# A quantiser's scale search beside a GRU recurrence: four groups of four scales, one for each step, without GpSimd

## The reference

```python
# layer 0: h from a GRU over the 32 steps, then attention on h, then a ternary-weight FFN
def cell(h, x):
    gi = x @ W_ih + b_ih
    gh = h @ W_hh + b_hh
    r = sigmoid(i_r + h_r); z = sigmoid(i_z + h_z)
    n = tanh(i_n + r * h_n)
    return (1.0 - z) * n + z * h

# layer 1, last part: both weights quantised to 5 bits, in blocks of 64 along the input
SHRINKS = np.linspace(0.4, 1.0, 16)
def mse_quant_dequant(w):
    amax = max(|wb|) per block;  base = max(amax, 1e-8) / 15
    for s in SHRINKS:
        scale = base * s
        deq = clip(round(wb / scale), -15, 15) * scale
        err = sum((deq - wb) ** 2)          # per block; the scale with the least error is kept
    return clip(round(wb / best_scale), -15, 15) * best_scale
```

## Time and profile before

| | us |
|---|---|
| median of 3 runs | 1633.81 (1633.55 to 1635.8) |
| the profiled execution | 1636.86 |
| its span | 1634.7 |

### The profile page before, as it was taken

The page is one execution under the profiler, slowest core; times in us unless marked ns, Lnnn a source line. Parts: engine busy times, 40 slices in busy tenths (PEclk is TensorE's granted clock), DMA queues, the critical chain, the costliest instruction groups (busy, mean ns, idle before and its releaser), DMA issues.

```text
span 1634.7 us, 24270 instructions
## 1 busy us (share of the span) xinstructions
PE 1419.8 (87%) x7971; PEld 1003.5 (61%) x7986; DVE 1108.2 (68%) x2613; ACT 867.6 (53%) x1772; POOL 367.8 (22%) x287
## 2 busy tenths in 40 slices
PE   5888888877998989899999886878889898989897
PEld 2333333345786877777777674555667585766766
DVE  3788888861455656564646668848686867678685
ACT  3877776756657565656666555443443424343311
POOL 2655554521211212121212100000102020110102
PEclk9999998888999999999999997979899999999999
DMA  9222222214110101010111131000000000000000
GB/s 368 53 52 52 52 77 52 52 53 147 52 33 26 40 26 39 26 38 26 38 38 61 40 136 65 1 26 7 13 8 13 6 13 6 13 7 7 14 7 13
DMA packets 26019, 73.45 MB, mean 45 GB/s; under 512 B 3928, under 2 KB 4700, under 8 KB 24544
## 3 DMA queue, kind: packets, MB, share of 16 engines
q1 hardware_dynamic: 25520, 71.67, 13.8%
q10 hardware_dynamic: 432, 0.92, 0.2%
HBM read 49.50 MB, written 23.07 MB: 44 GB/s over the span
## 4 chain that ended last, share of the span: by engine, by line
PE 37%; issue 20%; DVE 13%; ACT 5%; POOL 5%; POOLq 0%; DVEq 0%; ACTq 0%
PE psum L924 8%; PE psum L895 6%; POOL stats L1710 4%; PE psum L573 4%; PE psum L934 3%; DVE work L1809 2%; PE psum L680 2%; PE psum L619 2%; ACT probs_t L1507 2%; PE psum L841 2%; PE psum L606 1%; PE psum L875 1%; PE psum L987 1%; PE psum L907 1%; PE psum L848 1%
## 5 line engine op out<-in xcount | busy, mean ns | idle before, releaser
L573 PE MATMUL psum<-h_all,w_big 128*128 (+1 forms) x1024 | 246.2, 387 | 6.6 <-ACT ident_bf L1218 4.9
L573 PEld LDWEIGHTS psum<-h_all,w_big 128*128 128x128 f32 x1024 | 190.4, 193 | 43.1 <-issue 14.0
L1710 POOL TENSOR_TENSOR stats<-stats,minus_half 128x32 f32<-128x32 f32 x15 | 103.5, 6902 | 369.3 <-ACT stats L1251 369.3
L1809 DVE SCALAR_TENSOR_TENSOR work<-work,taps 128x248 f32<-128x248 f32 (+30 forms) x558 | 151.1, 349 | 0.0
L531 PE MATMUL psum<-w_big,h_all 128*64 128x512 f32 x512 | 133.0, 643 | 0.0
L924 PE MATMUL psum<-w_big 128*128 128x256 f32 x448 | 114.8, 416 | 20.1 <-ACT w_big L1536 20.1
L924 PEld LDWEIGHTS psum<-w_big 128*128 128x128 f32 x448 | 92.6, 210 | 42.2 <-ACT w_big L1536 26.6
L1809 DVE SCALAR_TENSOR_TENSOR h_all<-h_all,taps 128x248 f32<-128x248 f32 (+30 forms) x434 | 116.0, 344 | 0.0
L895 PE MATMUL psum<-work,w_big 128*128 128x256 f32 x512 | 115.8, 379 | 0.0
L680 PE MATMUL psum<-w_big,gru_mem 128*128 128x256 f32 x512 | 113.6, 379 | 0.0
L1679 POOL TENSOR_TENSOR work<-work,ffn_mem 128x512 f32<-128x512 f32 x60 | 85.6, 1458 | 95.2 <-DVE work L1876 90.1
(11 more groups left out here) (283 smaller groups left out, 2830.2 us busy)
## 6 DMA issues: line engine op xcount, KB each, us to landing
value_rows<-w_emb SPq DMA_DIRECT2D x128, 128.0 KB, 2.3
work<-value_rows SPq DMA_DIRECT2D x16, 1024.0 KB, 5.6
w_big<-in_Wq SPq DMA_DIRECT2D x2, 2048.0 KB, 16.7
w_big<-in_Wo SPq DMA_DIRECT2D x2, 2048.0 KB, 21.0
out<-w_big SPq DMA_DIRECT2D x16, 256.0 KB, 2.0
x_res<-out SPq DMA_DIRECT2D x15, 256.0 KB, 2.7
work<-in_w SPq DMA_DIRECT2D x1, 2048.0 KB, 11.7
w_big<-in_Wv SPq DMA_DIRECT2D x1, 2048.0 KB, 18.8
```

Source lines behind the costliest of these rows:

```text
L573: mm = pe.matmul(bank(n % 2)[:, o * TA:(o + 1) * TA], w_big[:, s, k * H * HD + at:k * H * HD + at + HD], h_all[:, k, bass.ds(i * BA, BA), ...
L1710: pool.tensor_tensor(qk_r, qk_ms, minus_half[:, 0:2 * GA * HU], ALU.pow).then_inc(r_on.sem, 1)
L1809: ins = dve.scalar_tensor_tensor(dst[:, :, lag:], src[:, :, :T - lag], tap, dst[:, :, lag:], ALU.mult, ALU.add)
```

## The change

The 16 scales are tried in four groups of four, so that each GRU step begins a group; group n (of 32) is raised in step n, rounded and subtracted in step n+1, squared in step n+2 and summed in step n+3. All 16 subtractions are VectorE's one-operation kind, all squares are ScalarE's; `scaled` and `squared` are gone, and GpSimd keeps `times_base` and `times_scale`. `w5_abs` has two buffers, `w5_tmp` four. `piece_out` is cut into five parts that are spread over steps 2, 3 and 0; parts 1 and 3 stand between the candidate's argument and the wait for its tanh. `piece_in(0)` comes before the first step's update, with a DMA of its own for the first eighth of w5, and a wait for the rest and for the constants (const_in) follows the first step. The hardware loops of three engines become straight code. The last two pieces of w5, not the last alone, are worked in gru_mem. The two bf16 constants are made in step 4. After the recurrence the last squares stand between the copies of projections, the raw weights are loaded earlier (the third when all errors are summed), and the three sums of absolute values come before `chunk(0)`, into scratch.

```diff
-GROUPS = (range(0, 6), range(6, 11), range(11, 16))
-BY_DVE = (2, 1, 1)
+GROUP = 4
+NG = NS // GROUP
+GROUPS = PIECES * NG
-W5_PARTS = (0, 4), (4, 7), (7, 8)
+W5_PARTS = (0, 4), (4, 6), (6, 8)
...
@@ SyncE
-            sp.dma_start(w5, io["w5"]).then_inc(w5_in, 16)
+            sp.dma_start(w5[:, 0:PC], io["w5"][:, 0:PC]).then_inc(w5_first_in, 16)
+            sp.dma_start(w5[:, PC:], io["w5"][:, PC:]).then_inc(w5_in, 16)
...
-            for pair in (T // 2 - 2, T // 2 - 1):
-                store_values(pair)
+            store_values(T // 2 - 2)
+            sp.wait_ge(h_on.sem, T)
+            sp.wait_ge(h_kept.sem, T)
+            for j, src in enumerate(("w_gate", "w_up", "w_down")):
+                if j == 2:
+                    sp.wait_ge(shr_err.sem, GROUPS)
+                sp.dma_start(raw[j], io[src]).then_inc(raw_in, 16)
+            store_values(T // 2 - 1)
             for j in range(2):
                 sp.wait_ge(v_out[j], 16 * T * V_TILES // 2)
+            load_values(0, 0, 0)
             sp.dma_start(w_emb[:], io["W_emb"]).then_inc(emb_in, 16)
-            sp.wait_ge(shr_err.sem, 3 * PIECES - 2)
-            load_values(0, 0, 0)
+            sp.dma_start(x_in_buf, io["x_tok"][:, 0:GA, :]).then_inc(x_in, 16)
             store_w5(2)
-            sp.wait_ge(h_on.sem, T)
-            sp.wait_ge(h_kept.sem, T)
-            for dst, src in zip(raw, ("w_gate", "w_up", "w_down")):
-                sp.dma_start(dst, io[src]).then_inc(raw_in, 16)
-            sp.dma_start(x_in_buf, io["x_tok"][:, 0:GA, :]).then_inc(x_in, 16)
@@ ScalarE
+            def raised(n, parts):
+                q, g = n // NG, n % NG
+                if 0 in parts:
+                    act.wait_ge(shr_pre.sem, q + 1)
+                    if q:
+                        act.wait_ge(shr_err.sem, n - NG + 1)
+                for j in parts:
+                    ins = act.activation(w5_tmp[g][:, j, :], w5_abs[q % 2], ACT.Identity, bias=magic_col[:],
+                                         scale=float(1.0 / SHRINKS[g * GROUP + j]))
+                if GROUP - 1 in parts:
+                    ins.then_inc(shr_raised.sem, 1)
+
+            def squares(n):
+                act.wait_ge(rest_on.sem, n + 1)
+                act.activation(w5_tmp[n % NG], w5_tmp[n % NG], ACT.Square).then_inc(sq_on.sem, 1)
+
+            for t in range(T):
+                u = t - 1
+                act.wait_ge(hid_sum.sem, t + 1)
+                act.activation(gates, bank(t % 2)[:, RZ], ACT.Tanh, scale=0.5).then_inc(rz_on.sem, 1)
+                if t:
+                    raised(t, range(0, 1))
+                act.wait_ge(cand_in.sem, 2 * t + 2)
+                act.activation(cand, cand, ACT.Tanh).then_inc(cand_on.sem, 1)
+                if u >= 2:
+                    keep_values(u // 2 - 1, u % 2)
+                if t:
+                    raised(t, range(1, 2))
...
+                if t == 0:
+                    absolute(0)
+                    raised(0, range(0, 2))
+                raised(t, range(2, GROUP))
+                if t >= 2:
+                    squares(t - 2)
+                if t % NG == NG - 1 and t < T - 1:
+                    absolute(t // NG + 1)
+                if t == NG:
+                    act.wait_ge(const_in, 16 * 5)
+                    act.activation(mask_bf[:], mask, ACT.Copy)
+                    const_on.raised_by(act.activation(ident_bf[:], ident[:], ACT.Copy))
...
-            act.wait_ge(shr_err.sem, 3 * PIECES - 1)
-            keep_qk(0, range(QK_TILES))
+            keep_qk(0, range(0, 2))
+            squares(GROUPS - 2)
+            keep_qk(0, range(2, 4))
+            squares(GROUPS - 1)
+            keep_qk(0, range(4, QK_TILES))
+            act.wait_ge(raw_in, 16 * 3)
+            sum_raw(0)
             keep_values(T // 2 - 1, 0)
+            act.wait_ge(shr_err.sem, GROUPS)
             keep_sums(0)
+            sum_raw(1)
             keep_values(T // 2 - 1, 1)
-            act.wait_ge(shr_err.sem, 3 * PIECES)
+            sum_raw(2)
             chunk(0, False, False)
@@ GpSimd
+            for q in range(3):
+                times_base(q)
+            for q in range(3, PIECES):
+                times_scale(q - 3)
+                if q >= late:
+                    pool.wait_ge(hid_sum.sem, (q - late + 1) * PC // B + 1)
+                times_base(q)
+            for q in range(PIECES - 3, PIECES - 1):
+                times_scale(q)
@@ VectorE
+            def errors(n):
+                g = n % NG
+                dve.wait_ge(sq_on.sem, n + 1)
+                dve.tensor_reduce(err[:, g * GROUP:(g + 1) * GROUP, :].rearrange("p s b -> p (s b)"),
+                                  blocks(w5_tmp[g].rearrange("p j n -> p (j n)")), AX.X, ALU.add).then_inc(shr_err.sem, 1)
+
+            def round_off(n):
+                q, g = n // NG, n % NG
+                dve.wait_ge(shr_raised.sem, n + 1)
+                dve.tensor_scalar(w5_tmp[g], w5_tmp[g], MAGIC + QMAX, MAGIC, ALU.min, ALU.subtract).then_inc(shr_cut.sem, 1)
+                dve.wait_ge(shr_cut.sem, n + 1)
+                for j in range(GROUP):
+                    tmp = w5_tmp[g][:, j, :]
+                    ins = dve.scalar_tensor_tensor(tmp, w5_abs[q % 2], -float(1.0 / SHRINKS[g * GROUP + j]), tmp,
+                                                   ALU.mult, ALU.add)
+                ins.then_inc(rest_on.sem, 1)
+
+            for t in range(T):
+                u = t % 2
+                q = t // NG
+                if t == 0:
+                    dve.wait_ge(w5_first_in, 16)
+                    piece_in(0)
+                dve.wait_ge(rz_on.sem, t + 1)
...
+                if t % NG == 3 and q >= 1:
+                    piece_out(q - 1, 1)
+                elif t % NG == 0 and q >= 2:
+                    piece_out(q - 2, 3)
...
+                if 3 <= t < T - 1:
+                    errors(t - 3)
+                if t:
+                    round_off(t - 1)
+                if t == 0:
+                    dve.wait_ge(w5_in, 16)
+                    dve.wait_ge(const_in, 16 * 5)
...
+                if t % NG == 0 and q >= 2:
+                    piece_out(q - 2, 4)
+                if t % NG == 1 and q < PIECES - 1:
+                    piece_in(q + 1)
+                if t % NG == 2 and q >= 1:
+                    piece_out(q - 1, 0)
+                if t % NG == 3 and 1 <= q < PIECES - 1:
+                    piece_out(q - 1, 2)
+            round_off(GROUPS - 1)
+            errors(GROUPS - 4)
+            errors(GROUPS - 3)
...
-            errors(PIECES - 1, 2)
-            dve.wait_ge(w5_on.sem, PIECES - 1)
-            piece_out(PIECES - 1)
+            for part in range(2, 5):
+                piece_out(PIECES - 2, part)
+            errors(GROUPS - 2)
+            errors(GROUPS - 1)
+            for part in range(5):
+                piece_out(PIECES - 1, part)
             chunk(0, False, False)
```

296 lines of the change are left out of this document (76 added, 220 removed).

## The result

| | before | after |
|---|---|---|
| median of 4 runs each, us | 1634.8 (1633.55 to 1640.75) | 1564.43 (1561.26 to 1571.89) |
| the profiled execution, us | 1636.86 | 1571.89 |
| its span, us | 1634.7 | 1570.1 |
| first operation of step 4 | 54.15 | 46.91 |
| a piece, (step 28 less step 8) / 5 | 41.3 | 35.02 |

The ratio is 0.9569 with a 95% interval of 0.9526 to 0.9612.

The account below looks back on a forecast made before the run. VectorE's queue was taken to bound the GRU stage, much of its busy time being stretching beside GpSimd. Gains of 46.1 us (stage) and 8.1 (hand-over), together 54.2, gave a median of 1579.6 us, range 1570 to 1598.

Parts of the forecast that it names:

- VectorE's own work: GRU stage: VectorE's undisturbed queue takes 7.71 us a step plus 4.4 a piece, 35.2 us a piece.
- the price of GpSimd's remaining work: GRU stage: each of GpSimd's two remaining products a piece delays VectorE 0.4 us, making 36.0 us a piece.
- my low end: Whole kernel: 1570 us, with remaining GpSimd work free (5.6 less) and no wait for the weights (3.7 less).
- The start: First GRU steps: base and GpSimd's product precede step 0; step 1 at 25.4 us, step 4 at 48.0.
- TensorE's pace: Rival, GRU stage: TensorE's clock falls in each step, making it 9.4 us; 11 us more, 1591; chance 0.11.
- waits for instructions in the straight code: Rival, former loops on three engines: instruction waits of 0.6 us over 32 steps, 19 us, 1599; chance 0.05.
- The hand-over: GRU stage to attention: outputs 59.2 us after the last state instead of 67.3, a gain of 8.1 us.
- an empty hand-over: Rival, hand-over: no gain, as ScalarE waits for raw weights with score copies queued behind; 1588; chance 0.13.
- From profile to median: Whole kernel: span 1580.5 us, execution 1582.7, median 1579.6, keeping the profiled span's 3.0 above the median.
- both small terms: Low end's two savings: remaining GpSimd work free, 5.6 us less; no hand-over wait for weights, 3.7 less.
- the end of the stretching: GRU stage: VectorE operations no longer lengthened beside GpSimd; pieces fall from 41.0 to 36.0 us, stage gain 46.1.

Follow-up runs that it names:

- The gaps experiment: Kernel after with the base's small operations and the selection's last part before the tanh wait, two raw-weight sums freed from the third weight: 1566.89 us, ratio 0.957.
- the six traces: Profiled executions of variants with the kernel after's hand-over and all its differences: outputs 55.6 to 59.3 us after the last state.
- The swap alone: Kernel before with all 16 differences on VectorE and all squares on ScalarE; groups of 6, 5, 5, start and hand-over unchanged: 1617.25 us, ratio 0.9891.
- the loaded-GpSimd run: Kernel after plus four GpSimd products of 512 columns, reading scratch memory, in each of 31 steps: 1656.46 us (one execution).

## Why the prediction came out too slow

The mechanism and the order of its parts held. Each step of the forecast beside the profiled execution of after, us:

| step of the forecast | forecast | measured |
|---|---|---|
| step 1 begins | 25.4 | 23.70 |
| step 4 begins | 48.0 | 46.91 |
| piece 1 | 34.3 | 33.84 |
| pieces 2 to 6, each | 36.0 | 35.02 |
| step 28 to the last state ready | 27.7 | 27.1 |
| last state | 290.0 | 283.0 |
| scores after it | 32.6 | 33.9 |
| outputs after it | 59.2 | 57.5 |
| span | 1580.5 | 1570.1 |

**VectorE's own work** was right. 7.71 us a step and 4.4 a piece make 35.2 against 35.02, and the prices (0.69 a difference, 1.22 a cut, 2.28 a reduction, 0.29 an update operation) are those forecast. The run with half of the differences shows that this queue sets the pace.

**The step that failed first is the price of GpSimd's remaining work**, 0.4 us for each product, 0.8 a piece. It cost nothing: 35.02 with the products and 35.02 without. I put the product's start 0.2 us behind the end of the step and its end at 1.25, and took the one caught operation of the earlier trace rows as typical. It starts 0.05 us behind the update's first operation and ends 1.09 behind it, 0.1 after the third begins at 0.99. The gaps experiment shows that the price does exist 1.0 to 1.4 us later in the step, 0.72 us each. It is a question of place, and 0.4 lies between the two prices and holds at neither place. Pieces 2 to 6 make 4.9 of the 10.4 us by which the span was overestimated; pieces 1 and 7, with the same term in part, 1.0. This is the largest single part of the 15.2 us between 1579.6 and 1564.4, but not half of it, and my low end had already put it at nothing.

**The start** was 1.1 us early at step 4. The forecast took step 2 to 3 as undisturbed, 7.7 us; it took 8.3 with a short fall of the clock, 12.2 with a long one, 6.6 with none. The forecast had TensorE's pace as a rival for the whole stage; it decides only in the first four steps, where VectorE has no errors to sum yet, and there 6.5 us lie between no fall and the long one. From 100 to 200 us the clock is 1.00, so that rival is refuted for the rest. So is the one of waits for instructions in the straight code: VectorE's queue is 92% busy, and a piece takes what its operations add up to. Against TensorE's pace I had argued that it rests less (1.3 us a step) than before any fall; that argument doesn't hold in the first steps, where rests of 1.38 and 0.48 us stood before a fall.

**The hand-over** gave 9.8 us, not 8.1. The projections came 0.6 later than forecast. ScalarE stood for w_down from 20.7 to 23.5 us after the state, where I had reckoned 20.4 to about 24. (The terms that I added to 18.8 for its issue make 18.6, and it was issued at 18.7.) The last values, said to be due only at the first outputs, were not free: two value copies waited 0.38 and 1.77 us for stores queued behind that weight. So the scores were 1.3 late. From the scores to the outputs it took 23.6 instead of 26.6 us; in other executions of kernels with this hand-over it was 22.9 to 25.7, so this term is not steady. From state to outputs the six traces have 55.6 to 59.3 us, and my 59.2 lies at their upper end. The part with the sums is shown by moving them back, in the traces alone (60.7 against these); the rival of an empty hand-over, 67.3, falls.

**From profile to median.** The span's error is 7.0 (stage) + 1.7 (hand-over) + 1.7 (rest of the program, which I had left as it was). That gives 1569 by the forecast's own reckoning. The last 5 us are that I gave the profiled execution of after the same 3.0 us above its median as that of before; it lay 7.5 above the median of its four, and 4.3 above that of all 16. Its untouched part took 1229.6 us, where the two other profiled executions of the same kernel had 1221.3 and 1218.0. This is spread of single executions and no mechanism of the change. The low end, 1570, assumed both small terms at their best, but nothing for the start, the rest of the program and the spread of executions, and that is why the range missed; over 16 executions the kernel after stands at 1567.6, outside too.

**What I hadn't separated.** The forecast let the gain in the stage come from the end of the stretching. The swap alone, with stretching gone and 7.2 us a piece of new differences on VectorE, brings the last state from 336.1 to 318.9, a third of the stage's 53 us. Of the other 36, 9.0 are there by step 4 (55.93 against 46.91; no run has the new start alone), and 26.9 come after it, where a piece goes from 38.95 to 35.02 by the even groups and the selection's parts in the gaps, which no run separates. Adding up one engine's queue gave the right sum because the new order is even. In the uneven order VectorE's queue without its waits for the gates is 36.4 us a piece, so the same sum would have been 1.8 us short in most pieces and 2.6 on average. Both parts are needed: the loaded-GpSimd run has the even order and is slower than before.

## What to carry to other kernels

Add up an engine's queue at prices read where its neighbours are idle, but only after looking whether each step has the same share: in a chain of steps the light step is held by the next engine, and the heavy one by this one. Before pricing a GpSimd operation beside VectorE, lay it on the timeline against the kinds of VectorE instructions: under PSUM readers, reductions and gaps it was free, 1.0 to 1.4 us later it cost 0.72, and one wait that held it under a reduction brought this back. And give a range room for the spread of executions, here 17 us between 16 of them, much of it in a part that the change leaves alone; take both sides of a comparison on the same chip.

## What the runs showed of the hardware

A GpSimd that only writes (memset) left VectorE's two-input operations at 0.29 and 0.69 us and stretched the cut of 2048 columns from 1.22 to up to 2.36 us; one that reads stretched both (0.94, 0.90 and 1.41 us on average). The Trainium skill (SBUF — State Buffer, "Who interferes with whom") says that two-input instructions contend with GpSimd's reads and not with its writes, and that `tensor_scalar` in a two-port mode contends with GpSimd at all. These numbers agree (that the cut runs in such a mode the traces don't say), and I should have priced the cuts by it before expecting 1572 at most.

TensorE's granted clock fell to 0.50 in the first steps in six of ten profiled executions with the same rests before it, and not in the four others, and stayed there for 7 us in one and 17 in another, worth up to 6.5 us at step 4.
